# The second half's grouped convolution by channel group, in 32 by 32 tiles of the array

## What is computed

```python
def _L0_cond_ref(x, c, weight, c_weight, bias):      # weight (32, 8, 9): 4 groups of 8 channels, 9 taps
    out = lax.conv_general_dilated(x, weight, window_strides=(1,), padding=[(4, 4)],
                                   dimension_numbers=('NCH', 'OIH', 'NCH'), feature_group_count=4)
    ctx = jnp.einsum('nd,od->no', c, c_weight)
    return out + ctx[:, :, None] + bias[None, :, None]
# _L0_ffn_ref on that: h = relu(x @ up_w) ** 2;  h @ down_w
#   + ((x @ fc1_w @ expert_w) * sum of the two largest gate logits) @ fc2_w;  then a layer norm
x = x + _L0_ffn_ref(_L0_cond_ref(...), ...)
# _L1_cond_ref: h = gelu(emb @ W0 + b0); h = gelu(h @ W1 + b1); att = softmax(h @ W2 + b2)
#   agg_w = einsum('bk,koi->boi', att, weight); out = einsum('boi,bih->boh', agg_w, x) + (att @ bias_k)
# _L1_ffn_ref: x @ W.T, and q, k, scores, softmax, A and Bm of 8 experts
x = x + _L1_ffn_ref(_L1_cond_ref(...), ...)
```

## Time and profile before

| | us |
|---|---|
| median of 3 runs (lowest, highest) | 217.27 (217.12, 217.29) |
| the profiled execution: time, its span | 217.51, 215.7 |
| PE, PEld busy | 211.2, 183.4 |
| DVE, ACT, POOL busy | 124.8, 80.1, 61.8 |
| the second half's convs on PE (96 records) | 78.62 to 89.25 |
| up(8), the first matmul of the second half's net | 92.10 |

### The profile page before, as it was taken

One profiled execution on the slowest core, in us unless ns is written; L12 is line 12 of the kernel. 1 busy time (PEld: TensorE's weight loads), 2 busy tenths in 40 slices (PEclk: granted clock), 3 DMA queues, 4 the chain that ended last, 5 costly groups with the idle time before them and its releaser, 6 DMA issues.

```text
span 215.7 us, 3106 instructions
## 1 busy us (share of the span) xinstructions
PE 211.2 (98%) x1155; PEld 183.4 (85%) x1155; DVE 124.8 (58%) x265; ACT 80.1 (37%) x156; POOL 61.8 (29%) x77
## 2 busy tenths in 40 slices
PE   7999899999999999999999999999999999999994
PEld 7997778888887789987888888888998998999984
DVE  4979356869525455597852034456996537435443
ACT  5998555369384612222222034431013112121110
POOL 3018421340475620021960012442264202202000
PEclk9999999999999999999999999999999999999999
DMA  6999655310000000174645000000000110110104
GB/s 177 346 406 406 219 116 109 61 27 0 0 3 0 0 0 3 25 123 68 91 41 146 0 0 0 3 0 2 0 3 0 49 49 3 50 49 0 52 0 146
DMA packets 31455, 14.94 MB, mean 69 GB/s; under 512 B 25336, under 2 KB 26168, under 8 KB 31440
## 3 DMA queue, kind: packets, MB, share of 16 engines
q1 hardware_dynamic: 30624, 14.05, 23.4%
q10 hardware_dynamic: 816, 0.69, 1.5%
HBM read 12.62 MB, written 2.11 MB: 68 GB/s over the span
## 4 chain that ended last, share of the span: by engine, by line
PE 95%; DVE 4%; issue 0%; DVEq 0%
PE PS L1214 26%; PE PS L1216 25%; PE PS L1215 25%; PE PS L1233 9%; PE PS L1341 3%; PE PS L1403 2%; DVE up_lo L864 1%; DVE H_lo L885 1%; PE PS L1258 1%; PE PS L1257 1%; PE PS L1412 1%; PE PS L1370 0%; PE PS L1267 0%; DVE ex_lo L997 0%; DVE up_hi L993 0%; PE PS L1456 0%
## 5 line engine op out<-in xcount | busy, mean ns | idle before, releaser
L910 DVE TENSOR_TENSOR PS<-PS,relu 128x512 f32<-128x512 f32 x16 | 11.2, 699 | 30.9 <-ACT relu L675 30.9
L1214 PE MATMUL PS<-H_hi,up_hi 128*128 128x512 f32 x64 | 25.6, 399 | 0.5 <-DVE H_lo L885 0.5
L1216 PE MATMUL PS<-H_hi,up_lo 128*128 128x512 f32 x64 | 25.0, 390 | 0.0
L1215 PE MATMUL PS<-H_lo,up_hi 128*128 128x512 f32 x64 | 25.0, 390 | 0.0
L1233 PE MATMUL PS<-wconv,XS 128*128 128x128 f32 x192 | 22.4, 276 | 0.0
L1233 PEld LDWEIGHTS PS<-wconv,XS 128*128 128x128 f32 x192 | 21.9, 192 | 0.3
L1216 PE MATMUL PS<-qkT_hi,H_lo 128*128 128x320 f32 x64 | 19.8, 309 | 0.0
L1215 PE MATMUL PS<-qkT_lo,H_hi 128*128 128x320 f32 x64 | 19.8, 309 | 0.0
L1214 PE MATMUL PS<-qkT_hi,H_hi 128*128 128x320 f32 x64 | 19.7, 308 | 0.0
L675 ACT ACTIVATE relu<-PS 128x512 f32<-128x512 f32 x16 | 9.5, 594 | 25.5 <-PE PS L1216 23.0
L595 POOL TENSOR_TENSOR X<-X,rowb 128x512 f32<-128x512 f32 x8 | 10.3, 1297 | 28.1 <-PE PS L1341 28.1
(11 more groups left out here) (187 smaller groups left out, 459.6 us busy)
## 6 DMA issues: line engine op xcount, KB each, us to landing
up_raw<-in_L_ffn_up_w_dram SPq DMA_DIRECT2D x2, 1024.0 KB, 8.9
dn_raw<-in_L_ffn_down_w_dram SPq DMA_DIRECT2D x2, 1024.0 KB, 13.0
out_dram<-X SPq DMA_DIRECT2D x7, 256.0 KB, 2.0
X<-in_x_dram SPq DMA_DIRECT2D x1, 1024.0 KB, 13.9
XS<-in_L_ffn_W_dram SPq DMA_DIRECT2D x16, 64.0 KB, 2.3
X<-in_x_dram SPq DMA_DIRECT2D x2, 256.0 KB, 2.9
X<-in_x_dram SPq DMA_DIRECT2D x1, 512.0 KB, 5.4
fc<-in_L_ffn_fc_w_dram SPq DMA_DIRECT2D x1, 512.0 KB, 5.7
```

The source lines that it names most:

```text
L910: nc.vector.tensor_tensor(U[i % 2], U[i % 2], relu[:], ALU.mult).then_inc(s_sq, 1)
L1214: nc.tensor.matmul(o, lh, rh, start=start, stop=False)
L1215: nc.tensor.matmul(o, lh, rl, start=False, stop=False)
L1216: return nc.tensor.matmul(o, ll, rh, start=False, stop=stop)
```

## The change

The second half's convs are done by channel group. For them XS holds, on 32 partitions g, the channel group g as (phase, channel in the group) for all 16 samples, and `wgrp` (128 by 3 by 32) the weights of each group as (phase, output channel in the group). One matmul takes a 32 by 32 block of weights as the stationary operand and 512 positions (four samples) as the moving one; its input partitions are those of group g, its output partitions those of sample block t. 3 windows by 4 blocks by 4 groups are 48 matmuls, in fp32 as before. Their results have the channels on the partitions; ACT copies two banks and DVE two to SBUF (`wide`), and 16 transposes (`turn_groups`) bring them into the old layout, with a tile T now made of sample s of each block (`of_sample`). XS is filled by the DMA queue: ACT and DVE copy X into phases (`phases`, two copies of 128 by 512 each) in place of the 16 slices' copies, 16 DMAs write them to `xph_rows` in DRAM and 16 read them back; 16 small DMAs make `wgrp` from `wconv`.

`wide` takes the memory of B1 and BD, which are filled after the convs now. The conditioning is moved ahead by two chunks and its bias matmul gets a place of its own, since the group convs write U[0], U[1], M[0] and M[1] at once and wait for all of its results. down(6) stands behind the group convs, before the transposes. The copy of fc2's high part goes from ACT to DVE.

```diff
+            sp.wait_ge(s_wconv, NWIN)
+            for g in range(G):
+                for j in range(PH):
+                    sp.dma_start(wgrp[C * g + CG * j:C * g + CG * (j + 1)].rearrange("k a (p o) -> k (a p) o", o=CG),
...
             for i, w in enumerate((L1_ffn_Wq, L1_ffn_Wk)):
                 load_blocks(qk_raw[:, :, i], w, ld_qk)
+            sp.wait_ge(xs_v, 10)
+            sp.wait_ge(xs_a, 7)
+            for t in range(TPH):
+                for s in range(SPT):
+                    sp.dma_start(xph_rows[:, :, t, s, :].rearrange("j c m -> c j m"),
+                                 wide[C * s:C * (s + 1), t].rearrange("c (j m) -> c j m", j=PH)).then_inc(s_xpw, 16)
+            sp.wait_ge(s_xpw, 16 * TPH * SPT)
+            sp.wait_ge(s_conv, TPH)
+            for g in range(G):
+                for j in range(PH):
+                    sp.dma_start(XS[C * g + CG * j:C * g + CG * (j + 1), :, 1:1 + P],
+                                 xph_rows[j, CG * g:CG * (g + 1)].rearrange("c t s m -> c (t s) m")).then_inc(ld_xs, 16)
             sp.wait_ge(s_conv, TILES)
...
+            pool.wait_ge(s_conv, TILES)
+            nc.gpsimd.memset(BD, 0.0).then_inc(s_zero, 1)
             pool.wait_ge(s_zero, 3)
...
-            act.wait_ge(ld_fc2, 16)
-            nc.scalar.activation(fc2_hi, fc2[:], ACT.Copy).then_inc(s_fc2h, 1)
...
                 if h:
-                    for t in range(TPH):
-                        split_H(TPH + t)
+                    act.wait_ge(s_grp, 1)
+                    for g in range(2):
+                        nc.scalar.activation(wide[:, g], conv_bank(TPH + g), ACT.Copy).then_inc(s_ga, 1)
+                    for s in range(SPT):
+                        split_H(TPH + s)
...
-                        if c in (5, 6):
-                            hidden(c - 5)
-                        if c == 7:
+                        if c in (3, 4):
+                            hidden(c - 3)
+                        if c == 5:
                             exp_att()
+                        if c == 6:
+                            copy_attT()
...
+            dve.wait_ge(ld_fc2, 16)
+            nc.vector.tensor_copy(fc2_hi, fc2[:]).then_inc(s_fc2h, 1)
...
                 if h:
-                    split_attT()
-                    copy_aggb()
-                    turn_agg()
+                    dve.wait_ge(s_grp, 1)
+                    for g in range(2, G):
+                        nc.vector.tensor_copy(wide[:, g], conv_bank(TPH + g)).then_inc(s_gv, 1)
                     for T in range(TPH, TILES):
                         add_ctx(T)
                         split_H(T)
...
-                    if h == 0 and c == 7:
+                    if h == 0 and c == 5:
                         att_scores()
                         att_weights()
+                    if h == 0 and c == 6:
+                        split_attT()
+                    if h == 0 and c == 7:
+                        turn_agg()
...
                     if h == 0 and c == 3:
-                        shift_copies(3)
-                    if h == 0 and c == 5:
+                        dve.wait_ge(ld_x[3], 16)
+                        nc.vector.tensor_copy(*phases(0))
+                        nc.vector.tensor_copy(*phases(1)).then_inc(xs_v, 1)
+                    if h == 0 and c == 4:
                         split_wk()
+                    if h == 0 and c == 7:
+                        copy_aggb()
...
+            def group_convs():
+
+                pe.wait_ge(ld_wgrp, 16 * G * PH)
+                pe.wait_ge(ld_xs, 16 * G * PH)
+                pe.wait_ge(s_R, IC)
+                pe.wait_ge(s_lat, LC)
+                pe.wait_ge(s_agg, 2)
+                pe.wait_ge(s_aggb, 1)
+                for a in range(NWIN):
+                    for t in range(TPH):
+                        for g in range(G):
+                            gs = slice(C * g, C * (g + 1))
+                            last = nc.tensor.matmul(conv_bank(TPH + g)[C * t:C * (t + 1), :], wgrp[gs, a],
+                                                    XS[gs, t * SPT:(t + 1) * SPT, a:a + P],
+                                                    start=(a == 0), stop=(a == NWIN - 1))
+                last.then_inc(s_grp, 1)
+
+            def turn_groups():
+
+                pe.wait_ge(s_ga, 2)
+                pe.wait_ge(s_gv, 2)
+                for s in range(SPT):
+                    view = conv_bank(TPH + s).rearrange("m (q g o) -> m g q o", g=G, o=CG)
+                    for g in range(G):
+                        last = nc.tensor.transpose(view[:, g], wide[:, g, s * P:(s + 1) * P], ident[:])
                     last.then_inc(s_conv, 1)
...
+            def mixing_bias():
+
+                pe.wait_ge(s_R, IC - 1)
+                nc.tensor.matmul(U[0][0:N, 0:C], attT2[:], bk[:],
+                                 start=True, stop=True).then_inc(s_aggbp, 1)
+
             def conditioning(c):
 
-                if c == 2:
+                if c == 0:
                     pe.wait_ge(ld_cond, 16 * 7)
+                    pe.wait_ge(s_lat, LC)
                     nc.tensor.matmul(M[0][:, 0:N], W0, cT[:, 0], start=True, stop=True).then_inc(s_c1p, 1)
...
             for h in range(HALVES):
                 if h:
-                    conv(TPH)
-                    for t in range(1, TPH):
-                        conv(TPH + t)
+                    group_convs()
+                    down(IC - 2)
+                    turn_groups()
                     down(IC - 1)
...
-                for c in range(IC if h else IC - 1):
+                for c in range(IC if h else IC - 2):
                     down(h * IC + c)
```

79 lines of the change are left out of this document (44 added, 35 removed).

## The result

| | before | after |
|---|---|---|
| median, us (runs) | 217.25 (217.12 to 217.29) | 228.22 (227.53 to 229.23) |
| ratio, with its 95% interval | | 1.051 (1.047 to 1.055) |
| profiled execution, us (span) | 217.51 (215.7) | 227.53 (225.8) |
| granted clock, mean of the profiled execution | 1.0 | 0.977 |

The change makes the kernel 10.97 us slower. The sign was forecast and the time lies in the range, but the size was not forecast: +3.7 us had been worked out.

A forecast was written before the change was run, and what follows sets the result against it. PE, busy for 98% of the span, was taken as the bound: 6.2 us of work saved against 9.95 us of new waits gave +3.7 us, 221.0 us against the median, range 218.5 to 229.5.

The forecast's parts named there:

- The sign: Whole kernel: slower, with chance 0.94; faster by more than 0.2% had 0.04, within 0.2% had 0.02.
- convs removed, group convs, transposes: PE's work in the second half's convs: -10.63 us removed, +3.5 for group convs, +1.8 for 16 transposes.
- wait at L1540: First conditioning matmul, now ahead of up(3): PE stands still for both latents, +4.3 us.
- attention weights: At turn_att, behind up(5) and down(3): a new PE wait of 1.0 us, bounds 0 and 2.
- before the group convs: DVE's copy of the bias needs R of chunk 7 and L1532: PE waits +0.35 us.
- wait before up(8): PE waits while DVE and ACT work off the four banks of H one after another: +4.3 us.
- start: fc2's copy on DVE lets POOL start earlier, so PE reaches up(0) earlier: -0.9 us, bounds 0 and 1.0.
- clock behind the two long waits: Matmuls after the waits at L1540 and before up(8): the sum took the clock as kept, no cost.
- rival 2: The two long waits cool PE's clock, costing 1.8 us each time: 222.8 or 224.6 us; chance 0.20.
- overlap of the tiles: Group convs: all 16 tiles stream together, so 96 records take 3.5 us; no overlap would be 42.5 us.
- the loads cost nothing: XS's DMAs before the group convs: landed at 75.0, PE asks at 81.3, 6 us of slack, no cost.
- Rival 3: The group convs' loads are late because each small DMA costs 0.9 us instead of 0.52: 227 us; chance 0.04.

The follow-up runs named there:

- e5: Kernel after, with 17 dummy fp32 matmuls that nobody reads in each of PE's two long waits: 225.36 us, 1.036 of the kernel before.
- e6: Kernel before, with only fc2's copy moved from ACT to DVE: 220.38 us, 1.015 of the kernel before.
- e7: Kernel after, with the loop over the three windows innermost in the group convs, six records in a row per tile: 240.36 us, 1.106 of the kernel before.
- e2: Kernel after, with the first conditioning matmul behind down(1), as in the kernel before: 228.06 us, its four runs between 223.01 and 230.84.
- e4: Kernel after, with fc2's copy on ACT, the first conditioning matmul behind down(1) and DVE's reordered H loop together: 224.76 us, 1.031 of the kernel before.
- e3: Kernel after, with DVE's order for the second half's H changed, two add_ctx ahead of the first split_H: 223.28 us, 1.030 of the kernel before.
- f1: Kernel after, with POOL's run of operations at the start held until DVE's small cast is done: 229.45 us, 1.055 of the kernel before.
- h2: h1 with the other 7 wgrp DMAs issued on SyncE's queue behind the phases' reads: 219.69 us, 1.009 of the kernel before.
- h1: e4 with 9 of wgrp's 16 DMAs issued from ACT's queue in its idle gaps: 219.88 us, 1.012 of the kernel before.
- f2: Kernel after, with phases written 128 partitions at a time and read back in 4 DMAs of 32 partitions: 230.79 us, 1.062 of the kernel before.

## Why the prediction was wrong in size

Step by step, by the profiles (forecast, measured):

| step | forecast | measured |
|---|---|---|
| convs removed, group convs, transposes | -5.3 | -10.63 + 3.33 + 1.66 = -5.6 |
| wait at L1540 | +4.3 | +4.24 |
| attention weights | +1.0 | +0.68 |
| before the group convs | +0.35 | +0.36 |
| wait before up(8) | +4.3 | +4.09 |
| start | -0.9 | +1.58 |
| clock behind the two long waits | 0 (rival 2: 1.8 a time) | +2.4 + 0.2 + 1.6 = +4.2 |
| the rest | | +0.6 |
| sum | +3.7 | +10.1 |

Most of the rest is in the waits too: what one costs is the distance between starts, 4.40 and 4.25 us for the two of 4.24 and 4.09.

Two terms make the miss. The clock: the sum left it at nothing and gave rival 2, which had it, 0.20 and 1.8 us a time. It was true both times, as e5 shows by taking it away, and at 2.6 and 1.6 us. What I had held against it, the 9 in the first slice of the clock's row, says nothing: the trace of the kernel before has no record of the clock ahead of 5.87 us, and the 14 slow matmuls end before that. The start: a term of the sum, -0.9, with bounds 0 and 1.0. It came out at +1.58, outside its bounds, because I priced the copy's move by what DVE would gain and did not ask what POOL, released 1.2 us earlier (14.78 against 16.02), would run into; e6 shows it alone, at some 3 us in the kernel before. The gain that I had seen was there (both L864 take 1.28 us instead of 2.79), but it came behind a loss of 2.2 us at L1318. The median of the kernel after lies 10.97 above, 0.9 more than its profile; that remainder is not settled.

Right were the sign, the overlap of the tiles (3.33 for 3.5), both long waits and the two short ones, with the releasers that I had named. The Trainium skill's figure for this ("TensorE: Matmul & The Clock Gate", section "Part 3: Packing small matmuls — row/col tiling"), 10.6 times for 16 tiles, gave 4.0 us as an estimate; by my 42.5 us for no overlap the trace shows 12.8 times. That page's other rule, starts and ends in program order, is in line with e7, where the order alone makes 16.07 us out of 3.33, but does not give that number. The Trainium skill's rule on idle gaps (the same page, section "HAM oscillation — how this bites in real kernels") agrees with both dents in the clock, behind 4.24 and 4.09 us idle.

Right by luck was that the loads cost nothing: they landed at 85.1, not at 75.0, and PE asked at 85.3 and not at 81.3, because the clock and the start had made it late. The 6 us of slack that I had worked out were 0.2. The kernels with shorter waits or without the slow clock, e2 to e5, then all ran into them. Rival 3 was the next bound in line, and a chance of 0.04 was too low for it.

## What to carry to other kernels

When PE is the bound, price each new standstill of some microseconds as itself plus a stretch of matmuls at half the clock behind it (1.5 to 2.6 us more here), and keep it short by DVE's order or fill it with matmuls that nobody reads. When an operation moves from one engine to another, follow the instruction that it releases: if that one runs on GpSimd, look for what VectorE is about to do at that moment. And a load that is hidden behind a wait must be priced as if the wait were gone: a new order on DVE brought 4.9 us of the 10.97 by itself, and together with the other edits it came to 8.5, but only with earlier loads: without them the three edits of e4 brought no more than e3's alone. No kernel here came below the one before.

## What the runs showed of the hardware that I had not expected

- A cast of 0.17 us on VectorE took 3.80 and 4.70 us when GpSimd had begun 0.06 and 0.04 us before, and lasted through four and five of GpSimd's operations, memsets included. A tensor_tensor with both inputs in SBUF was held for 2.1 us only, while GpSimd's subtraction ran (f1).
- After 4.24 us without work PE ran about 5 us at the lower clock, after 4.09 us about 3 (the kernel after), after 4.13 us 3.4 (e3) and after 3.30 us 3.4 (e6's profile). After 1.7 us (e3) and 2.40 us (L1318 of the kernel after) it did not fall. In e4 and h2, after 9.48 and 3.37 us of waiting, all or nearly all of the group convs ran at it (5.13 and 5.93 us by their rows), in h1, after 4.23 us, about 3 us of them (4.87). In e2, e5 and f2, after waits of 2.9, 1.9 and 2.4 us for the same loads, their records had the full rate (587 ns). So a longer wait did not cost more.
- PE worked almost without a gap from 1.1 us on, and the clock rose to its upper level at 4.0 to 5.9 us in nine of the fourteen profiles and at 9.4 to 10.7 in the other five. The profile's page and windows show 1.00 there, since no record of the clock stands ahead of that rise.
- 16 DMAs of 8 partitions took 11.8 us (3 KB each) and 11.1 us (64 KB each) to issue; 4 DMAs of 256 KB, 32 partitions each, took 9.2 us. The 16 of 64 KB moved 1 MB at 60 GB/s, the 4 of 256 KB at 78 with half the share of busy engines.
